# A two-layer transformer kernel: shared tokens in transposed form, keys of several batches in one product, and a re-written order of work

## The chip, the cores and the metric

The kernel runs on one core of one Trainium2 chip. The metric is the device time of one launch in microseconds (us). The core has five engines that run side by side and tell each other by semaphores what is done: TensorE (PE, matrix products, weight loads shown as PEld), VectorE (DVE), ScalarE (ACT), GpSimd (POOL) and SyncE (SP), which here issues every transfer. Each engine works through its own list strictly in the order in which the list was written.

## The reference

```python
xn = layernorm(x)                                   # x: 8 batches x 256 tokens x 128
x  = x + attention(xn, Wq, bq, Wk, bk, Wv, bv, Wo, bo) + experts(xn, Wg, w1, w2)
xn = layernorm(x)
x  = x + state_space(xn, W_in, conv, A, D, W_x, W_dt, W_out) + ffn(xn, w1, w2, h1, h2, w3)
# attention: 16 query heads, 4 key/value heads of 8 columns, softmax over 256 keys
# experts: gates from xn @ Wg, top two of 8; all experts have the same w1 (128x512), w2
# state_space: 4 taps, silu, dt = softplus, and over 512 tokens a row, 16 states a channel:
#   h = h * exp(-A * dt) + B;  y = sum(h) + D * x;  y * silu(z) @ W_out
# ffn: silu(x @ w1.T) * (x @ w2.T), two 512x512 layers with gelu, one 512x128
```

## The kernel before

The first layer (function `layer0`) goes batch by batch, b = 0 to 7, with 256 tokens each. The second (`layer1`) goes group by group, g = 0 to 3, with 512 tokens each. What an engine does is cut into named pieces, and the table `ORDERS` says for each engine in which order the pieces stand; `S` in the tensor list is the next score piece, `A` the next one of the second kind, and so on. There is no scheduler: the tables are the order.

A batch of the first layer takes these pieces on TensorE, by their lines in the kernel before: `xn_transposes` (L444) turns the normalised tokens; `project` (L457 queries, L460 keys) multiplies them by Wq and by Wk; `v_gate` (L431) makes values and gate numbers; 16 `S` pieces (L328, L317 for the first half of batch 0) make scores whose row maxima VectorE takes (`M`, L589); `max_rows` (L423) turns the maxima; 16 `A` pieces (L342) make the scores again, transposed and with the maxima taken off inside the product; ScalarE turns each into probabilities (`E`, L548); four `pv` pieces (L357) multiply them by the values; `heads`, `back` and `proj_out` (L374, L408, L414) bring the result back; `ffn_in` and `ffn_out` (L388, L396) are the experts. Queries and keys are cut into three bfloat16 parts that are written to memory (`put`, L242 and L245) and read back in another layout (`fetch`, L255 and L259, for `S`; `stack`, L283, for `A`). The parts are made by ScalarE (`qk_out`, L521 and L522: four instructions a batch) and GpSimd (`qk_split`, L692 to L695: three). `warm` (L451) are products that nobody reads.

In the second layer `x_in` (L933), `ffn` (L885, L886), `second` (L896), `third` (L908) and `out` (L970, L980) are the large products of a group. For each of 16 states ScalarE makes two decays (`D`, L1088), TensorE spreads the input (`b`, L869), VectorE does two recurrences (`scan`, L1163) and GpSimd adds both to a sum (`add`, L1218). GpSimd closes a group with `y` (L1226), which `out` reads.

Two of the eight banks in which products land serve `S`, two serve `A`, one `pv`. The other three, bA, bB and bC, are shared: bA has the turned tokens in its left half and the two projections in its two halves, bB the experts, bC values, turned maxima and the way back. Before it writes such a bank, each piece waits until the former content is read.

Of the kernel before, what the change touches and what calls it, by code (L numbers as in the profile page):

```python
# [65 lines left out]
def settled(eng, sem, v):  # L66
# [6 lines left out]
    sync="""2*x_in head ffn_weights constants0 x_in 3*put fetch stack 3*put fetch stack 3*put 3*rows fetch loads 2*put  # L73
        rows put 2*rows loads stack fetch 3*rows stack 3*put fetch loads 3*rows 3*put fetch stack 3*rows 3*put fetch
        stack 3*rows put stack 2*put fetch 3*rows stack 3*rows b_rows loads b_rows 2*out 2*b_rows 6*out landed""",
    tensor="""9*warm xn_transposes 4*warm project ffn_in v_gate 6*warm ffn_in 2*S warm xn_transposes S project ffn_out 2*S
        warm S xn_transposes 2*S 4*warm 2*S warm project 2*S 5*warm 2*S 5*warm 2*S warm ffn_in warm max_rows 2*S
        warm ffn_in v_gate 2*S warm ffn_out A S A S 2*warm A S warm A S warm xn_transposes A S A S project 2*S pv S
        2*A S A S A S ffn_in max_rows A S A S pv A S A S pv A S A S ffn_in A S A S pv A S A S v_gate heads ffn_out A
        S xn_transposes back A S A S project S A S pv A S proj_out A S A S max_rows pv A S A S A S v_gate A S A S pv  # L80
        A S A pv A 2*S A heads ffn_in A S A S back ffn_in A S A S pv A S A S xn_transposes proj_out ffn_out max_rows
        A S A S pv A S A project A S A S pv S v_gate A S A S pv A 2*S A heads ffn_in A S A S pv A S A S back ffn_in
        proj_out A S A S xn_transposes ffn_out max_rows A S A S pv A S A S project v_gate ffn_in A S A S pv A S A S
        pv A S A S ffn_in A S A S pv A S A S heads ffn_out back A S A S proj_out xn_transposes A S A S max_rows
        project A S A 2*pv A 2*S A v_gate A S pv A S A S ffn_in A S A S heads A S pv A S A S ffn_in A S A S back
# [1264 lines left out]
```

## Time and profile before

| | us |
|---|---|
| median of three runs (lowest, highest) | 371.38 (370.75, 372.19) |
| span of the profiled execution, first to last instruction | 370.3 |
| the profiled execution's own time outside the span | not listed apart; median less span is 1.1 |
| TensorE busy | 361.6 |
| ScalarE busy | 314.4 |
| VectorE busy | 303.1 |
| GpSimd busy | 238.0 |

A busy TensorE is not a TensorE at its peak: products are pipelined and overlap in the profile. How long a piece really holds the engine is the distance from its start to the start of the next one where nothing is waited for.

### The profile page before, as it was taken

How to read it: one execution, taken by the hardware profiler on the slowest of the kernel's cores; microseconds unless marked ns; L12 is line 12 of the kernel's file. 1: busy time of each engine (PE TensorE's matmuls, PEld its weight loads, DVE VectorE, ACT ScalarE, POOL GpSimd, SP SyncE). 2: the span in 40 equal slices, each digit the busy share in tenths (PEclk: the TensorE clock that was granted, in tenths of full speed). 3: DMA queues.
4: the chain of work that ended last, by engine and by line, in shares of the span. 5: the costliest groups of instructions: out<-in, count | busy, mean ns of one | idle time of the engine just before them, and what ended most of it. 6: DMA issues, size and time to landing. Idle time of an engine off the chain costs nothing.

```text
span 370.3 us, 5874 instructions
## 1 busy us (share of the span) xinstructions
PE 361.6 (98%) x1810; PEld 185.9 (50%) x1810; DVE 303.1 (82%) x508; ACT 314.4 (85%) x540; POOL 238.0 (64%) x287
## 2 busy tenths in 40 slices
PE   7999999999999999999999999999999999999996
PEld 6757454546454553433324445465445464464546
DVE  4786879978788888579878768989999989998950
ACT  4934878886988887899998899999999999799870
POOL 2156504642527211342989673999999999999990
PEclk9999999999999999999969999999999999999999
DMA  6477282746265220220000000001000000000000
GB/s 217 125 145 147 93 200 35 174 143 120 58 110 123 43 55 2 52 85 0 1 21 3 1 0 2 0 0 48 5 0 21 0 3 28 1 2 1 0 28 28
DMA packets 29902, 19.63 MB, mean 53 GB/s; under 512 B 4496, under 2 KB 28848, under 8 KB 29616
## 3 DMA queue, kind: packets, MB, share of 16 engines
q1 hardware_dynamic: 29872, 19.26, 21.3%
q8 instruction: 14, 0.23, 0.3%
q14 instruction: 16, 0.13, 0.1%
HBM read 13.69 MB, written 5.37 MB: 51 GB/s over the span
## 4 chain that ended last, share of the span: by engine, by line
PE 68%; ACT 8%; DMA 2%; issue 2%; DVE 2%; SPq 0%; POOL 0%; ACTq 0%; DVEq 0%; POOLq 0%
PE bank L908 15%; PE bank L896 13%; PE bank L357 6%; PE bank L980 4%; PE bank L342 4%; ACT da L1088 3%; PE bank L869 3%; PE bank L885 3%; PE bank L886 3%; PE bank L953 3%; PE bank L933 3%; PE bank L388 2%; PE bank L328 2%; PE bank L396 2%; PE bank L970 2%; ACT pt L548 2%
## 5 line engine op out<-in xcount | busy, mean ns | idle before, releaser
L1218 POOL TENSOR_TENSOR acc<-acc,hb 128x512 f32<-128x512 f32 x128 | 158.1, 1273 | 11.6 <-DVE hb L1163 11.2
L1163 DVE TENSOR_TENSOR_SCAN hb<-da,bank 128x512 f32<-128x512 f32 x128 | 145.9, 1200 | 15.1 <-PE bank L869 9.1
L589 DVE TENSOR_REDUCE mx<-bank 128x2 f32<-128x512 f32 x128 | 83.1, 683 | 16.9 <-PE bank L328 14.4
L1088 ACT ACTIVATE da<-dt,nega 128x510 f32<-128x510 f32 x128 | 82.2, 713 | 0.2
L548 ACT ACTIVATE pt<-bank 128x512 f32<-128x512 f32 x128 | 71.2, 596 | 9.8 <-PE bank L342 8.7
L896 PE MATMUL bank<-sil,ld 128*128 128x512 f32 x128 | 59.1, 595 | 0.0
L908 PE MATMUL bank<-gelu,ld 128*128 128x512 f32 x128 | 58.5, 593 | 0.1
L342 PE MATMUL bank<-q_st,k_st 51*128 51x512 bf16 x128 | 42.2, 386 | 1.8 <-ACT pt L548 1.5
L328 PE MATMUL bank<-k_st,q_st 48*128 48x256 bf16 x240 | 38.9, 273 | 0.1
L896 PEld LDWEIGHTS bank<-sil,ld 128*128 128x128 f32 x128 | 24.3, 192 | 26.3 <-issue 25.7
L908 PEld LDWEIGHTS bank<-gelu,ld 128*128 128x128 f32 x128 | 23.8, 190 | 25.6 <-issue 24.7
L357 PE MATMUL bank<-pt,v_sb 128*32 128x512 f32 x256 | 35.4, 632 | 0.0
L342 PEld LDWEIGHTS bank<-q_st,k_st 51*128 51x128 bf16 x128 | 9.4, 93 | 38.3 <-ACT pt L548 25.5
L869 PE MATMUL bank<-b_parts,sel 96*128 96x512 bf16 x64 | 24.3, 393 | 0.4 <-DVE hb L1163 0.4
L1088 ACT ACT_TABLE_LOAD x18 | 23.1, 1283 | 0.3
L1142 DVE SCALAR_TENSOR_TENSOR xc<-bank,ld,xc 128x510 f32<-128x510 f32 (+2 forms) x24 | 17.6, 743 | 3.5 <-ACT xc L1015 2.9
L328 PEld LDWEIGHTS bank<-k_st,q_st 48*128 48x128 bf16 x240 | 15.5, 94 | 8.5 <-DVE mx L589 4.8
L692 POOL TENSOR_TENSOR qk_parts<-qk,qk_parts 128x512 bf16<-128x512 f32 x7 | 8.1, 1156 | 16.2 <-ACT qk_parts L522 16.2
L388 PE MATMUL bank<-xnT,w 128*128 128x256 f32 x64 | 17.3, 392 | 0.0
L933 PE MATMUL bank<-xnT,ld 128*128 128x512 f32 x32 | 16.7, 607 | 0.5 <-DVE xc L1142 0.3
L980 PEld LDWEIGHTS bank<-ld,gelu 128*128 128x128 f32 x128 | 15.8, 192 | 2.4 <-issue 2.1
L885 PE MATMUL bank<-xnT,ld 128*128 128x512 f32 x32 | 16.5, 598 | 0.0
(148 smaller groups left out, 534.0 us busy)
## 6 DMA issues: line engine op xcount, KB each, us to landing
q_st<-q_scr SPq DMA_DIRECT2D x8, 384.0 KB, 4.9
q_st<-q_scr SPq DMA_DIRECT2D x15, 192.0 KB, 3.8
ld<-in_pack SPq DMA_DIRECT2D x2, 1024.0 KB, 6.3
q_scr<-qk_parts SPq DMA_DIRECT2D x8, 192.0 KB, 2.1
k_st<-k_scr SPq DMA_DIRECT2D x15, 96.0 KB, 4.5
q_scr<-qk_parts SPq DMA_DIRECT2D x8, 128.0 KB, 2.1
out<-x SPq DMA_DIRECT2D x8, 128.0 KB, 1.9
ld<-in_pack SPq DMA_DIRECT2D x1, 968.0 KB, 5.4
```

Of the source, the lines that this page charges most:

```text
L328: last = mm(s_bank[n % 2][:, j * T:(j + 1) * T], q_st[b % 2][0:ROWS, 2 * pair + j, q * P:(q + 1) * P], k_st[b % 2][0:ROWS, 2 * pair // G, ...
L342: mm(st(b, n)[:, :], k_st[b % 2][HALF:, kv, kt * P:(kt + 1) * P], q_st[b % 2][HALF:, h0:h0 + 2, :].rearrange("r h n -> r (h n)"), start=Tr ...
L357: last = mm(pv_bank[kv * VW:(kv + 1) * VW, :], v_sb[b % 2][:, kt, kv, at:at + VW], pt[:, (4 * grp + kv) % 8, :], start=(grp == 0), stop=(g ...
L548: act(pt[:, n % 8, :], st(b, n)[:, :], ACT.Exp, scale=HD ** -0.5).then_inc(p_ok, 1)
L589: eng.tensor_reduce(mx[:, 2 * pair:2 * pair + 2, q], s_bank[n % 2][:, :].rearrange("p (h k) -> p h k", h=2), AX.X, ALU.max).then_inc(mx_ok, 1)
L869: mm(b_bank(g, s)[:, :], sel[:, s, :], b_parts[:, g % 2, :], start=True, stop=True).then_inc(b_ps, 1)
L896: last = mm(f_bank(g, c)[:, :], h1[:, k, c * P:(c + 1) * P], sil[:, k, :], start=(k == 0), stop=(k == KC - 1))
L908: last = mm(f_bank(g, c)[:, :], h2[:, k, c * P:(c + 1) * P], g2[:, k, :], start=(k == 0), stop=(k == KC - 1))
L980: last = mm(out_bank(g, q)[:, r], g3[:, k, r], w3[:, k, :], start=False, stop=(k == KC - 1 and q == out_last(g, q)))
L1088: act(da(n)[:, :, 1:T], dt[:, g % 2, c, :].rearrange("p (b n) -> p b n", b=GB)[:, :, 1:T], ACT.Exp, scale=nega[:, c, s:s + 1]).then_inc(da ...
L1163: eng.tensor_tensor_scan(hb[:, s % NPAIR, c, :], da(n).rearrange("p b n -> p (b n)"), b_bank(g, s)[:, :], 0.0, ALU.mult, ALU.add).then_inc ...
L1218: TT(acc[:, g % 2, c, :], acc[:, g % 2, c, :], hb[:, s % NPAIR, c, :], ALU.add).then_inc(add_ok, 1)
```

## The change

The normalised and turned tokens of all eight batches now stay in the buffer `xnT1`, which the second layer fills later, so that their making can run ahead; `xn` has two buffers. The keys of batch 0, of batches 1 to 3 and of batches 4 to 7 are made by one piece each, `project_keys`: one product of 32 columns of weights for each batch, side by side in one bank. Key parts are made, cut and written for the whole group (`k_out`, `split_k`, `put_keys`), query parts for each batch (`q_out`, `split_q`, `put`). There are four value buffers instead of two. The semaphores of fetched data are kept apart for even and odd batches. Turned tokens and queries use the left half of one bank (`half0`), values, maxima and the way back the right half of another (`half1`); the two halves of the tokens' bank are no longer both used. Which content must be read before a shared bank is written stands in short tables (`X_AFTER` to `H_AFTER`). The first loads come in another order and size. All five lists of `ORDERS` are new. The score banks stay one bank for each piece, two in turn.

```diff
-    sync="""2*x_in head ffn_weights constants0 x_in 3*put fetch stack 3*put fetch stack 3*put 3*rows fetch loads 2*put
+    sync="""2*x_in head constants0 x_in ffn_weights put_keys 2*put 2*put_keys put fetch 2*put_keys 2*put put_keys put
...
+NV = 4
+KEYS = ((0,), (1, 2, 3), (4, 5, 6, 7))
+X_AFTER = "- q0 x1 x2 q1 q2 x5 x6"
+Q_AFTER = "x0 x3 x4 k2 q3 q4 q5 q6"
+KEYS_AFTER = "x7"
+V_AFTER = "- m0 m1 m2 m3 m4 m5 m6"
+M_AFTER = "v0 v1 v2 p1 p2 v5 p4 v7"
+T_AFTER = "v3 p0 v4 v6 p3 m7 h6 h7"
+P_AFTER = "t0 t1 t2 t3 t4 t5 t6 t7"
+F_AFTER = "- f0 f1 h1 h2 f4 h3 h4"
+H_AFTER = "f2 h0 f3 f5 f6 f7 p5 p6"
...
-    xnT = [sb(f"xnT_{p}", [P, T]) for p in range(2)]
-    xn = sb("xn", [P, TPB, P])
+    xnT = [t["xnT1"][:, b * T:(b + 1) * T] for b in range(NB)]
+    xn = [sb(f"xn_{p}", [P, TPB, P]) for p in range(2)]
...
-    X_PARTS = ((0, TPB), (TPB, 3 * TPB), (3 * TPB, NT))
+    bA, bB, bX = banks[5:8]
+    half0, half1 = bA[:, 0:T], bX[:, T:2 * T]
+    X_PARTS = ((0, TPB), (TPB, 4 * TPB), (4 * TPB, NT))
...
+    EMPTIED = dict(x=((xnT_ok, 1),), q=((q_ok, 1),), k=((k_ok, 1),), v=((v_ok, 1), (srt_ok, TPB)), m=((negm_ok, 1),),
+                   t=((oT_ok, 1),), p=((x1_ok, 1),), h=((on_ok, 1),), f=((y_ok, 1),))
+    def emptied(eng, before, n):
+        name = before.split()[n]
+        if name == "-":
+            return
+        for signal, per in EMPTIED[name[0]]:
+            eng.wait_ge(signal, per * (int(name[1:]) + 1))
...
+        def put_keys(n):
+            j, k = n // NRUN, n % NRUN
+            first, last = KEYS[j][0], KEYS[j][-1]
+            k_out = a["k_scr"][first:last + 1].rearrange("o p c n -> (o p) c n")
...
         def project(b):
             reached(eng, xnT_ok, b, 1, 1)
-            mm(bA[:, 0:T], wq[:, :], xnT[b % 2][:, :], start=True, stop=True)
+            emptied(eng, Q_AFTER, b)
+            mm(half0, wq[:, :], xnT[b], start=True, stop=True).then_inc(q_ps, 1)
...
-            mm(bA[:, T:2 * T], wk4[:, :], xnT[b % 2][:, :],
-               start=True, stop=True).then_inc(qk_ps, 1)
+        def project_keys(j):
+            reached(eng, xnT_ok, KEYS[j][-1], 1, 1)
...
+            for i, b in enumerate(KEYS[j]):
+                last = mm(key_bank(j)[32 * i:32 * i + 32, :], wk4[:, 0:NKV * HD], xnT[b], start=True, stop=True)
+            last.then_inc(k_ps, 1)
...
         def xn_out(b):
             reached(eng, xnT_ps, b, 1, 1)
-            reached(eng, f_ps, b - 2, 1, 1)
-            reached(eng, v_ps, b - 2, 1, 1)
-            act(xnT[b % 2][:, :], bA[:, 0:T], ACT.Copy).then_inc(xnT_ok, 1)
+            act(xnT[b], half0, ACT.Copy).then_inc(xnT_ok, 1)
...
-        def qk_out(b):
-            for half, bias in ((0, bq_c), (1, bk_c)):
+        def q_out(b):
+            if b > 0:
+                act(qk[:, 0:T], half0, ACT.Identity, bias=bq_c[:, 0:1])
+            act(qk_parts[:, 0, 0:T], half0, ACT.Identity, bias=bq_c[:, 0:1]).then_inc(q_ok, 1)
+        def k_out(j):
+            r = slice(0, NKV * HD * len(KEYS[j]))
+            if j > 0:
+                act(qk[r, T:2 * T], key_bank(j)[r, :], ACT.Identity, bias=bk_c[r, 0:1])
+            act(qk_parts[r, 0, T:2 * T], key_bank(j)[r, :], ACT.Identity, bias=bk_c[r, 0:1]).then_inc(k_ok, 1)
...
-            reached(eng, pv_ok, b - 2, 4, 4)
+            reached(eng, pv_ok, b - NV, 4, 4)
...
-        def qk_split(b):
-            TT(qk_parts[:, 1, :], qk[:, :], qk_parts[:, 0, :], ALU.subtract).then_inc(split, 1)
+        def split_q(b):
+            c = slice(0, T)
+            TT(qk_parts[:, 1, c], qk[:, c], qk_parts[:, 0, c], ALU.subtract).then_inc(q_split, 1)
```

Three places show how the lists move. The first is TensorE at the start of the second layer's share of batch 7; `L342` is the `A` piece, `L357` `pv`, `L933` `x_in`, `L885` and `L886` `ffn`. Before:

```order
L423 MATMUL bank<-head,mx 32x128
L342 MATMUL bank<-q_st,k_st 128x512 x2
L357 MATMUL bank<-pt,v_sb 32x512 x4
L342 MATMUL bank<-q_st,k_st 128x512
L357 MATMUL bank<-pt,v_sb 32x512 x4
L342 MATMUL bank<-q_st,k_st 128x512 x2
L933 MATMUL bank<-xnT,ld 128x512
```

After, where the same pieces are L402, L417, L1008, L959 and L960, and L461 and L468 are `back` and `proj_out`:

```order
L402 MATMUL bank<-q_st,k_st 128x512
L994 MATMUL bank<-head,xn 128x128 x4
L943 MATMUL bank<-b_parts,sel 128x512
L417 MATMUL bank<-pt,v_sb 32x512 x4
L402 MATMUL bank<-q_st,k_st 128x512
L1008 MATMUL bank<-xnT,ld 128x512 x2
L402 MATMUL bank<-q_st,k_st 128x512
L468 MATMUL bank<-cst,oT 128x128 x2
L417 MATMUL bank<-pt,v_sb 32x512 x4
L402 MATMUL bank<-q_st,k_st 128x512
```

The end of batch 5 (`back`, `proj_out`) and the `pv` pieces now stand between the `A` pieces of batch 7, which are spread more evenly.

The second place is ScalarE where the second layer's group 1 begins its recurrences; `da` is a decay `D`, `xc` the taps. Before:

```order
L1015 ACTIVATE xc<-bank,ld 128x512
L1088 ACT_TABLE_LOAD
L1088 ACTIVATE da<-dt,nega 128x2x255
L1015 ACTIVATE xc<-bank,ld 128x512
L1088 ACTIVATE da<-dt,nega 128x2x255
L1009 ACT_TABLE_LOAD
L1009 ACTIVATE sil<-bank,ld 128x512
```

After:

```order
L1090 ACTIVATE xc<-bank,ld 128x512 x2
L1084 ACT_TABLE_LOAD
L1084 ACTIVATE sil<-bank,ld 128x512
L1117 ACTIVATE xn<-x,nmean,rstd 128x128 x4
L1097 ACTIVATE zs<-bank 128x512
L1084 ACTIVATE sil<-bank,ld 128x512
L1097 ACTIVATE zs<-bank 128x512
L1084 ACTIVATE sil<-bank,ld 128x512
L1108 ACTIVATE xs<-xc 128x512 x2
L1084 ACTIVATE sil<-bank,ld 128x512
L1163 ACT_TABLE_LOAD
L1163 ACTIVATE da<-dt,nega 128x2x255 x2
```

The first two decays of group 1 moved behind the last `sil`, and one table load is gone there.

The third is GpSimd at the same place; `acc<-xs` is `start`, the other `acc` are `add`. Before:

```order
L1218 TENSOR_TENSOR acc<-acc,hb 128x512 x4
L1226 TENSOR_TENSOR y<-acc,zs 128x512 x2
L1210 TENSOR_TENSOR acc<-xs,ld 128x512
L1218 TENSOR_TENSOR acc<-acc,hb 128x512 x9
L1231 TENSOR_TENSOR b_rest<-b_full,b_cut 128x128
```

After:

```order
L1302 TENSOR_TENSOR y<-acc,zs 128x512
L1294 TENSOR_TENSOR acc<-acc,hb 128x512
L1286 TENSOR_TENSOR acc<-xs,ld 128x512
L1302 TENSOR_TENSOR y<-acc,zs 128x512
L1294 TENSOR_TENSOR acc<-acc,hb 128x512 x3
L1307 TENSOR_TENSOR b_rest<-b_full,b_cut 128x128
```

The `start` ahead of group 1's adds is now one of group 1 itself; before, it was one of group 2.

## Rows read from the trace of the kernel before

**Rows 1.** The page: busy times, 40 slices of the span, the chain by engine.

```profile
PE 361.6 (98%) x1810; PEld 185.9 (50%) x1810; DVE 303.1 (82%) x508; ACT 314.4 (85%) x540; POOL 238.0 (64%) x287
...
PEclk9999999999999999999969999999999999999999
...
PE 68%; ACT 8%; DMA 2%; issue 2%; DVE 2%; SPq 0%; POOL 0%; ACTq 0%; DVEq 0%; POOLq 0%
```

**Rows 2.** Timeline of TensorE: start, length, line, operation, shape, count, [idle before].

```profile
5.72 0.44 PE L444 MATMUL bank<-head,xn 128*128 128x128 f32 x2 [0.73 <-DMA head<-in_head]
...
14.59 0.59 PE L457 MATMUL bank<-xnT,head 128*128 128x256 f32 x2
15.02 0.59 PE L460 MATMUL bank<-xnT,head 128*128 128x256 f32 x2
...
30.06 0.27 PE L423 MATMUL bank<-head,mx 128*32 128x128 f32 x1
...
42.12 0.39 PE L342 MATMUL bank<-q_st,k_st 51*128 51x512 bf16 x1 [0.47 <-ACT pt L548]
...
46.41 1.06 PE L357 MATMUL bank<-pt,v_sb 128*32 128x512 f32 x8
47.41 0.39 PE L342 MATMUL bank<-q_st,k_st 51*128 51x512 bf16 x1
...
47.95 1.13 PE L388 MATMUL bank<-xnT,w 128*128 128x256 f32 x4
```

**Rows 3.** Timeline of TensorE: where batch 7 and the second layer's stages begin.

```profile
149.73 0.39 PE L342 MATMUL bank<-q_st,k_st 51*128 51x512 bf16 x1
...
186.92 0.61 PE L342 MATMUL bank<-q_st,k_st 51*128 51x512 bf16 x1 [0.15 <-ACT pt L548]
...
216.05 1.88 PE L933 MATMUL bank<-xnT,ld 128*128 128x512 f32 x4
...
361.97 1.95 PE L970 MATMUL bank<-wout_half,y 128*128 128x128 f32 x16
```

**Rows 4.** Busy time by stage: stretch, length, PE, PEld, DVE, ACT, POOL, clock.

```profile
149.70:186.90 37.20, 35.51 (x142) 13.62 (x141) 28.51 (x37) 36.12 (x63) 20.44 (x22) 0.98 0.11 34
231.90:361.70 129.80, 129.80 (x438) 66.07 (x436) 117.82 (x115) 122.65 (x167) 128.26 (x109) 1.00 0.03 10
...
188.00:190.00 2.00, 2.00 (x12) 0.39 (x8) 1.14 (x2) 1.97 (x3) 2.00 (x2) 0.50 0.22 49
```

**Rows 5.** Groups by line, ScalarE and GpSimd: busy, mean ns, idle before.

```profile
L522 ACT ACTIVATE qk_parts<-bank,cst 128x256 bf16<-128x256 f32 x16 | 7.5, 474 | 0.0
...
L1088 ACT ACT_TABLE_LOAD x18 | 23.1, 1283 | 0.3
```

**Rows 6.** Timeline of ScalarE around the end of batch 7 and at group 1.

```profile
39.91 0.47 ACT L521 ACTIVATE qk<-bank,cst 128x256 f32<-128x256 f32 x1
...
41.47 2.16 ACT L548 ACTIVATE pt<-bank 128x512 f32<-128x512 f32 x4
...
188.18 1.28 ACT L1069 ACT_TABLE_LOAD   x1
189.47 1.27 ACT L1069 ACTIVATE gelu<-bank,ld 128x512 f32<-128x512 f32 x2
...
219.20 0.72 ACT L1088 ACTIVATE da<-dt,nega 128x510 f32<-128x510 f32 x1
```

**Rows 7.** Timeline of GpSimd from group 1's adds on.

```profile
227.96 1.04 POOL L1210 TENSOR_TENSOR acc<-xs,ld 128x512 f32<-128x512 f32 x1 [8.41 <-ACT xs L1033]
...
231.93 8.65 POOL L1218 TENSOR_TENSOR acc<-acc,hb 128x512 f32<-128x512 f32 x7 [0.46 <-DVE hb L1163]
...
359.13 2.49 POOL L1226 TENSOR_TENSOR y<-acc,zs 128x512 f32<-128x512 f32 x2
```

**Rows 8.** The chain that ended last, around batch 6's fetch: start, length, what.

```profile
102.56 4.87 DMA q_st<-q_scr
```

**Rows 9.** Timeline of VectorE: the second pair of recurrences of group 1.

```profile
230.63 11.40 DVE L1163 TENSOR_TENSOR_SCAN hb<-da,bank 128x512 f32<-128x512 f32 x10 [1.26 <-ACT da L1088]
```

More of the change, by code:

```diff
@@ L72 @@
 ORDERS = dict(
-    sync="""2*x_in head ffn_weights constants0 x_in 3*put fetch stack 3*put fetch stack 3*put 3*rows fetch loads 2*put
[L74 to L85, printed above, removed]
-        ffn_out A S proj_out pv max_rows S A S A ffn_in A S A S pv A S v_gate A S A S pv A S A S ffn_in heads A S A
-        S pv S A x_transposes A S A S back ffn_out A S A S x_in proj_out x_in ffn max_rows 2*A pv A pv 2*A x_in ffn
-        x_in A wx A ffn 2*step_in ffn b A x_transposes pv A x_in b x_in A 2*second heads b A x_in A second x_in A b
-        second wx pv A b step_in back A pv A b step_in A b A proj_out 2*A b A 2*pv 2*b 2*second b second b second
-        heads b third back third proj_out b 2*third 2*b 3*third x_transposes third 2*x_in 2*ffn x_in 2*b x_in 2*ffn
-        out wx b 2*second b second b 2*second b second out b step_in b 2*second 2*b 3*out third b out x_transposes b
-        third x_in step_in 2*b 2*third b third b 2*third b x_in third x_in 2*ffn b x_in wx b 2*ffn step_in b out b
-        2*second b second b second b 2*second b second b second 2*out b out b 2*out third b third step_in b third b
-        third b third b third b 2*third b ffn b ffn out b ffn b ffn out b 2*out second b 2*second b second b second
-        b second b 2*second b 2*out b 2*third b 2*third b 4*third 6*out""",
@@ L119 @@
[L119 to L122 removed]
+    sync="""2*x_in head constants0 x_in ffn_weights put_keys 2*put 2*put_keys put fetch 2*put_keys 2*put put_keys put
+        fetch put stack 2*rows 2*put rows fetch loads stack put_keys 3*rows 2*put put_keys put loads fetch stack put
+        put_keys 2*put 3*rows 3*put fetch stack 3*rows fetch stack 3*put 3*rows fetch stack loads 3*rows 2*put stack
+        put fetch 3*rows stack 3*rows loads 2*b_rows 2*out 2*b_rows 6*out landed""",
@@ L302, in ffn_weights @@
             eng.dma_start(w12[:, :], a["w12"]).then_inc(ld_ffn, 16)
-        return dict(x_in=x_in, head=head, constants0=constants0, ffn_weights=ffn_weights, put=put, fetch=fetch, rows=rows,
+        return dict(x_in=x_in, head=head, constants0=constants0, ffn_weights=ffn_weights, put=put, put_keys=put_keys, fetch=fetch, rows=rows,
                     stack=stack, loads=loads)
@@ L1179, in clear @@
                 settled(eng, done["st_ps"], (NB - 1) * NH)
-                settled(eng, done["stk_ok"], 32 * NB)
+                for p in range(2):
+                    settled(eng, done["stk_ok"][p], 16 * NB)
                 settled(eng, done["y_ok"], NB)
```

323 lines of the change are left out of this document (183 added, 140 removed).

## The prediction, made before the changed kernel had run

> **What bounds the kernel now.** I read the page first, then TensorE's own timeline, then the busy time by stage, then the lists of ScalarE and GpSimd. On the page TensorE is busy for 361.6 of 370.3 us and makes up 68% of the chain that ended last, with its clock at 2.4 GHz but for one slice [rows 1]. A busy share hides how much of it is work, so I priced each piece by the distance from its start to the next start where nothing is waited for: one projection 0.43 us (14.59 to 15.02), `pv` 1.00 (46.41 to 47.41), and two `A` with two `S` beside them 0.54 (47.41 to 47.95), that is 0.21 for each pair and 0.1 for leaving the small-tile form [rows 2]. Pieces of `ffn_in`, `ffn_out` and the second layer are priced in the same way: 0.86 for each product of 512 columns in float32, 0.11 for one of 128. Multiplied by the pieces in the list before, this makes 348.3 us of work. The remaining 22 us of the span are idle time of TensorE or half-speed time, and they are what a new order can win.
>
> By stages, each ended by a row: the first `max_rows` at 30.06 [rows 2], the first `A` of batch 7 at 149.73, its last `A` at 186.92, `x_in` of group 2 at 216.05 and the last group's `out` at 361.97 [rows 3].
>
> - To 30.06: 26.1 us of work, 4.0 idle (the first loads; `xn_transposes` waits for a load until 5.72 [rows 2]).
> - To 149.73: 112.0 of work, 7.7 idle, in dozens of waits of 0.1 to 0.9 us.
> - To 186.92: 33.8 of work in 37.2. Here ScalarE is busy 36.1 of 37.2 us [rows 4]: it is the bound of this stage.
> - To 216.05: 26.2 of work, 2.9 lost, most of it at half clock: between 188 and 190 us the granted clock is 0.50 of full speed [rows 4], just after `A` pieces for which TensorE had waited for ScalarE, the last at 186.92 [rows 3].
> - To 361.97: 144.8 of work, 1.1 idle. TensorE is stall-free from about 232 on, but GpSimd is busy for 128.3 of the 129.8 us from 231.9 to 361.7 [rows 4]. Both are the bound: the last two `y` end at 361.62, and the `out` that reads them starts at 361.97 [rows 3, 7].
> - The last 8.3 us (24 products, an add, a transfer) don't change.
>
> **The change part by part.**
>
> *Keys.* Eight key projections of 0.43 us go (3.4 us of TensorE). Three groups of 1, 3 and 4 products of 32 weight columns come. The trace has no such product of 256 columns, but `pv` is four products of 32 columns side by side: eight passes in 1.00 us [rows 2], which one after the other would be at least four times 0.86. If key products overlap in the same way, the three groups cost 3 x 0.43 = 1.3; if not, 8 x 0.43 = 3.4, and nothing is won. I take 1.3, since the form of `pv` is the same. Range of the edit: -2.1 to 0.
>
> *Form changes.* Counting both lists, TensorE leaves or enters the small-tile form 146 times instead of 138, at 0.1 us: +0.8. The Trainium skill (TensorEngine Tiling (Array Packing), Key Properties) says that a change of tiling mode drains the engine while different tiles run in parallel; the trace agrees with both halves, at 0.1 us a change and with `pv` as above, and the first half speaks against this change. With the keys the work falls from 348.3 to 347.0.
>
> *ScalarE.* Four conversions a batch (0.47 us each, 0.36 apart) become two, and three groups of one or two are added. In the old order the four stand in a row between two `E`: they begin at 39.91, the next `E` at 41.47 [rows 6], and TensorE's `A` at 42.12 had waited for it [rows 2]. Seven such gaps of 1.5 us become 0.7. Of the table loads of 1283 ns [rows 5], 49 in the list before, 40 are left: 11.5 us less over the whole kernel. The Trainium skill (ScalarE: Activation LUTs, What ACT_TABLE_LOAD costs) adds a drain of about 1.38 us to each load, which would make 24 us; the trace doesn't show it here: the load at 188.18 is followed by its `gelu` at 189.47 [rows 6].
>
> *GpSimd and transfers.* Cutting goes from 3 x 1.16 us on 512 columns to three on 256 for each batch, and four `put` transfers a batch less are issued. In the old order batch 6's fetch landed at 107.43 [rows 8], while TensorE wanted it 0.3 us before. In the new one the queries of batches 4 to 7 are projected 25, 29, 26 and 22 us of work ahead of their scores (before 18, 14, 13 and 16). Price -0.5. On SyncE `rows` of batch 0 now stand behind two `put` of batch 2; these are due some 2 us before the maxima are, so I take 0, up to +1.
>
> *Start.* The second load of x grows from 256 to 384 KB ahead of the weights that `xn_transposes` waits for, and the experts' weights become the last load. I expect the first transposition near 6.2 instead of 5.72 and `ffn_in` near 9.6 instead of 8.2; the two stretches of `warm` ahead of it shrink by about as much. The first `S` comes at 11.3 to 12.0 (before 11.57). Price 0, -0.3 to +1.
>
> *Value buffers, parity semaphores.* Before, making values of batch b waited for `pv` of b-2, which cost VectorE 0.4 us in all. Hidden beside TensorE's work: 0.
>
> *New waits.* All small results now pass through two half banks. Behind each such wait stands the whole of TensorE's list. The distances in work between writer and next writer are at least 0.7 to 1.1 us at the tightest (values of batches 1, 3 and 7 after maxima, and `max_rows` of batch 6), about what the reads between them take (0.25 to 0.4 us and a handover). So 0 to 0.3 each, some 1 us in all.
>
> *Stage sums.* With the new list the stages hold 26.1, 107.9, 37.1, 25.7 and 144.8 us of work: four us move from the second stage past the first `A` of batch 7. For idle time I take 4.0 in the first stage. In the second, 6.0 (7.7 less 0.5 for the fetch, less about 2 for the shorter ScalarE rows, plus 1 for new waits). In the third, ScalarE's list between first and last `E` of batch 7 falls from 36.5 to 35.0 us, below TensorE's 37.1: TensorE becomes the bound, with 1.2 idle. In the fourth I take 1.6 instead of 2.9, half-way between keeping and losing the half-speed stretch, which cost about 2.5.
>
> In the fifth the end is set by GpSimd. The first two decays of group 1 move behind the last `sil`; they were made at 219.20, between the taps [rows 6]. By the chain taps, x_in, ffn, sil, table load (1.28), decay, I get the first recurrence of group 1 at 229.4 on the old clock instead of 225.75, the second pair at 231.7 instead of 230.63 [rows 9], and the first add at 230.6. From there GpSimd's list holds 132.5 us with no hole, so the last `y` ends at 363.1 instead of 361.6: +1.5. What is won is that the add no longer waits for group 2's `start`, which had cost 8.41 us of GpSimd idling until 227.96 [rows 7].
>
> Sum: 30.1 + 113.9 + 38.3 + 27.3 + (144.8 + 1.1 + 1.5) + 8.3 = 365.3 us of span, against 370.3. With the 1.1 us by which the median stands over the span: 366.4.
>
> **The rivals.**
>
> *More is won (20%).* The half-speed stretch goes altogether (-1.6) and the second stage loses only 4 us (-2): 362.8. For it: TensorE would no longer wait for ScalarE ahead of that stretch. Against it: `A` pieces still come one by one between waits.
>
> *Given back on GpSimd (18%).* Recurrences of group 1 start yet later, since the decays stand behind a `sil` that needs the last `ffn` product, and everything after is a full GpSimd list: each microsecond there is one of the end. With +3.5 instead of +1.5 and the second stage unchanged at 7.7: 370.1. This includes key products that don't overlap (+2).
>
> *The half banks bind (12%), slower.* `v_gate`, `max_rows`, `back` and `proj_out` share one half bank, each released by VectorE or ScalarE from the middle of its own full list. If VectorE comes 0.5 us late at three of them a batch, eight batches lose 12 us, less the gain of 5.0: 378. It decides from about 0.3 us a time on. For it: VectorE is busy for 303 of 370 us [rows 1], so a short read often stands behind longer work of its list. Against it: the shorter ScalarE rows let scores and probabilities, for which VectorE's list waits too, come on time more often.
>
> *The change doesn't do what it says.* If no piece ran earlier and only the work fell, 1.3 us are won: 370.1, within the second rival.
>
> **How the numbers follow.** Forecast 50%, its own range 363.8 to 369.0. A measurement of this kernel can tell 0.5%, or 1.9 us, from no change: faster means below 369.5. The forecast and the first rival lie there, and a third of the second's half-way cases, less the forecast's upper tail: 0.71. Within 0.5% lie most of the second rival and the mild form of the third: 0.18. Slower: 0.11. The range of 8 in 10 leaves out a tenth on either side: 362.3 to 373.0.
>
> **What would show it.** In the changed profile: key products of a group starting within about 0.1 us of each other, and each group done in some 0.45 us; the last `A` of batch 7 near 182; ScalarE less than fully busy in the stage before it; 40 table loads; no or a shorter stretch at 0.50 clock after it; the first add of group 1 near 225 and GpSimd without a hole from there to the last `y` near 357. Wrong, if TensorE's waits for `half1` (VectorE's copies and adds on the way back, the maxima) add up to over 3 us, if the first `A` of batch 7 comes after 147, or if GpSimd has new holes after group 1's first add.

## The result: slower by 1.2%, and the profile after

| | before | after |
|---|---|---|
| median (us) | 371.58 (370.75 to 372.19, 4 runs) | 375.97 (375.85 to 376.16, 4 runs) |
| ratio after to before | | 1.0124, 95% interval 1.0101 to 1.0146 |
| span of the profiled execution | 370.3 | 374.4 |
| its own time | not listed | 376.16 |

The forecast of 366.4 and its range (362.3 to 373.0) missed. The page of the changed kernel, answering to [rows 1]: ScalarE is relieved as forecast (314 to 298 us), but 15% of the chain that ended last is now "issue", time in which an engine in the chain waited for nothing that the profile shows.

```profile
PE 364.5 (97%) x1810; PEld 184.7 (49%) x1810; DVE 303.1 (81%) x514; ACT 298.0 (80%) x521; POOL 232.0 (62%) x293
...
PEclk9999999999999999999999999999989999999998
...
PE 61%; issue 15%; ACT 13%; POOL 6%; DVE 3%; POOLq 0%; ACTq 0%; DVEq 0%
```

The timeline of TensorE (start, length, line, operation, shape, count, what ended its idle time) shows where the stages of [rows 2, 3] end now, and two places that were not there before.

```profile
7.35 0.38 PE L492 MATMUL bank<-head,xn 128*128 128x128 f32 x2
...
16.78 0.63 PE L518 MATMUL bank<-xnT,head 128*32 128x256 f32 x6
17.34 1.12 PE L375 MATMUL bank<-hb,dt 128*128 128x512 f32 x2
...
31.18 0.27 PE L475 MATMUL bank<-head,mx 128*32 128x128 f32 x1
...
146.28 0.39 PE L402 MATMUL bank<-q_st,k_st 51*128 51x512 bf16 x1
...
185.10 0.39 PE L402 MATMUL bank<-q_st,k_st 51*128 51x512 bf16 x1
...
212.46 1.96 PE L1008 MATMUL bank<-xnT,ld 128*128 128x512 f32 x4
...
272.36 1.02 PE L960 MATMUL bank<-xnT,ld 128*128 128x512 f32 x2
275.69 1.23 PE L959 MATMUL bank<-xnT,ld 128*128 128x512 f32 x2 [2.31 <-DVE sil L1200]
276.71 1.92 PE L960 MATMUL bank<-xnT,ld 128*128 128x512 f32 x2
278.42 2.71 PE L1045 MATMUL bank<-wout_half,y 128*128 128x128 f32 x16
...
364.33 2.84 PE L1045 MATMUL bank<-wout_half,y 128*128 128x128 f32 x16 [1.91 <-POOL y L1302]
366.96 4.59 PE L1055 MATMUL bank<-ld,gelu 128*128 128x128 f32 x32
```

Stage by stage, in us:

| stage up to | before | forecast | after |
|---|---|---|---|
| first `max_rows` | 30.1 | 30.1 | 31.2 |
| first `A` of batch 7 | 119.7 | 113.9 | 115.1 |
| last `A` of batch 7 | 37.2 | 38.3 | 38.8 |
| `x_in` of group 2 | 29.1 | 27.3 | 27.4 |
| last group's `out` | 145.9 | 147.4 | 151.9 |
| end | 8.3 | 8.3 | 10.1 |

(The row names follow the prediction; the fourth ends with the `x_in` at 216.05 before and 212.46 after.) The gain of the first layer and of its seam came: 216.05 became 212.46. Then 3.6 us in hand became 4.1 us lost. Of that, 6.0 us went before the last `out` and 1.7 us behind it. About half of the 3.6 us is clock: the profiled execution of before has a half-speed stretch in the fourth stage that cost 1.8 us and that the same order does not always have (e5 below).

At the first new place TensorE waits for `sil`. ScalarE's timeline shows who held that up:

```profile
268.68 0.69 ACT L1084 ACTIVATE sil<-bank,ld 128x512 f32<-128x512 f32 x1 [0.15 <-PE bank L960]
273.15 0.60 ACT L1097 ACTIVATE zs<-bank 128x512 f32<-128x512 f32 x1 [3.79 <-POOL y L1302]
273.65 0.62 ACT L1108 ACTIVATE xs<-xc 128x512 f32<-128x512 f32 x1
274.17 0.68 ACT L1084 ACTIVATE sil<-bank,ld 128x512 f32<-128x512 f32 x1
```

`zs` is `gate_z` of group 3's first half. It writes a buffer that group 1's `y` reads, and its wait asks for both `y` of group 1. GpSimd's timeline has them late in a list without holes, and then holes:

```profile
269.21 1.27 POOL L1302 TENSOR_TENSOR y<-acc,zs 128x512 f32<-128x512 f32 x1
270.44 1.27 POOL L1294 TENSOR_TENSOR acc<-acc,hb 128x512 f32<-128x512 f32 x1
271.79 1.27 POOL L1302 TENSOR_TENSOR y<-acc,zs 128x512 f32<-128x512 f32 x1
...
277.44 1.27 POOL L1294 TENSOR_TENSOR acc<-acc,hb 128x512 f32<-128x512 f32 x1 [0.93 <-DVE hb L1238]
...
284.46 2.50 POOL L1294 TENSOR_TENSOR acc<-acc,hb 128x512 f32<-128x512 f32 x2 [1.07 <-DVE hb L1238]
288.06 1.27 POOL L1294 TENSOR_TENSOR acc<-acc,hb 128x512 f32<-128x512 f32 x1 [1.10 <-DVE hb L1238]
...
361.59 2.48 POOL L1302 TENSOR_TENSOR y<-acc,zs 128x512 f32<-128x512 f32 x2
```

The circle is closed: ScalarE waits for GpSimd's `y`, TensorE for the `sil` queued behind that wait, VectorE's recurrences for TensorE's `b`, GpSimd for the recurrences. Before the change the same `y` ended at about 273.5 and ScalarE came to the same `zs` at 273.89, so nobody waited:

```profile
271.04 2.48 POOL L1226 TENSOR_TENSOR y<-acc,zs 128x512 f32<-128x512 f32 x2
...
273.89 0.59 ACT L1022 ACTIVATE zs<-bank 128x512 f32<-128x512 f32 x1
```

GpSimd moved only 0.5 us forward (to 273.06), ScalarE 4.5 (to 269.36). Against an execution of the old order without the half-speed stretch (e5: `y` ends at 271.71, `zs` begins at 272.04) ScalarE moved 2.7 us forward and GpSimd 1.35 us back.

Both waits of TensorE are followed by slow products. Busy time by stretch (length, then PE, PEld, DVE, ACT, POOL, the granted clock as the sixth number, DMA share, GB/s):

```profile
275.60:282.90 7.30, 7.21 (x37) 5.63 (x38) 6.39 (x8) 6.92 (x8) 6.38 (x6) 0.77 0.00 0
364.30:371.00 6.70, 6.67 (x45) 6.70 (x46) 0.00 (x0) 0.00 (x0) 0.00 (x0) 0.75 0.00 0
```

Sixteen `out` records take 2.54 us from 278.42 to the next piece instead of the 1.78 that the same piece took before (361.97 to 363.75): part of them run at 1.2 GHz.

### The profile page after: what moved, and what is told of

Same layout as the page of the kernel before. It is cut to its first block, busy times and chain, and to the rows that moved or that the text cites. A ratio compares the mean times of both kernels' runs of the same rounds, so it can differ in the third digit from the quotient of the medians.

```text
span 374.4 us, 5851 instructions
## 1 busy us (share of the span) xinstructions
PE 364.5 (97%) x1810; PEld 184.7 (49%) x1810; DVE 303.1 (81%) x514; ACT 298.0 (80%) x521; POOL 232.0 (62%) x293
## 4 chain that ended last, share of the span: by engine, by line
PE 61%; issue 15%; ACT 13%; POOL 6%; DVE 3%; POOLq 0%; ACTq 0%; DVEq 0%
PE bank L970 7%; PE bank L417 7%; PE bank L402 5%; ACT da L1163 5%; POOL acc L1294 4%; PE bank L386 4%; PE bank L445 4%; PE bank L453 4%; PE bank L499 4%; PE bank L982 4%; PE bank L1055 3%; DVE hb L1238 2%; PE bank L960 2%; PE bank L959 2%; PE bank L1045 2%
## 5 line engine op out<-in xcount | busy, mean ns | idle before, releaser
L402 PE MATMUL bank<-q_st,k_st 51*128 51x512 bf16 x128 | 40.8, 383 | 0.3 <-ACT pt L612 0.3
L417 PE MATMUL bank<-pt,v_sb 128*32 128x512 f32 x256 | 34.1, 605 | 0.0
L402 PEld LDWEIGHTS bank<-q_st,k_st 51*128 51x128 bf16 x128 | 9.0, 93 | 36.4 <-ACT pt L612 25.9
L943 PE MATMUL bank<-b_parts,sel 96*128 96x512 bf16 x64 | 23.5, 382 | 0.1
L959 PE MATMUL bank<-xnT,ld 128*128 128x512 f32 x32 | 16.8, 605 | 2.3 <-DVE sil L1200 2.3
L1055 PEld LDWEIGHTS bank<-ld,gelu 128*128 128x128 f32 x128 | 17.1, 202 | 3.6 <-issue 3.4
L1055 PE MATMUL bank<-ld,gelu 128*128 128x128 f32 x128 | 17.2, 284 | 0.0
L960 PE MATMUL bank<-xnT,ld 128*128 128x512 f32 x32 | 17.2, 621 | 0.0
L499 PE MATMUL bank<-warm_in 128*128 128x256 bf16 x88 | 15.9, 317 | 1.4 <-DVE warm_in L622 1.4
```

The source lines that it names most:

```text
L402: mm(st(b, n)[:, :], k_st[b % 2][HALF:, kv, kt * P:(kt + 1) * P], q_st[b % 2][HALF:, h0:h0 + 2, :].rearrange("r h n -> r (h n)"), start=Tr ...
L417: last = mm(pv_bank[kv * VW:(kv + 1) * VW, :], v_sb[b % NV][:, kt, kv, at:at + VW], pt[:, (4 * grp + kv) % 8, :], start=(grp == 0), stop=( ...
L1055: last = mm(out_bank(g, q)[:, r], g3[:, k, r], w3[:, k, :], start=False, stop=(k == KC - 1 and q == out_last(g, q)))
```

## The experiments

**e1 and e5: the wait for `y`.** The same edit to the changed kernel and to the kernel before.

```diff
         def gate_z(g, c):
-            reached(eng, y_ok, g - 2, CI, CI)
+            reached(eng, y_ok, g - 2, CI, c + 1)
```

> One edit to the changed kernel: the gate z of group g waits only for the y of its own half that last read the buffer, not for both y of group g-2. Theory (the gain of the first layer is lost in the second, where ScalarE stands 3.8 us before zs at 273.15 for GpSimd's y): TensorE's idle 2.3 us at 275.69 and the slow products behind it (1.8 us) shrink to under 0.5 together, GpSimd's three holes of about 1 us each between 277 and 289 go, the last y ends near 361 instead of 364.07, and the span is 371 to 371.5 (time about 373). TensorE then waits longer for the last y, about 3 us instead of 1.9. Rival (the time was lost in the first layer on the shared half banks): span unchanged within 0.5 us.

> The kernel before the change with the same one edit as e1 (gate z waits only for the y of its own half). Theory (the wait costs only in the new order, in which ScalarE comes to zs at 269.4 while GpSimd's second y ends at 273.1; in the old order both met at 273.5 and 273.9): no change, span 370.3 within 0.5, ratio 1.00. Rival (the wait cost the old order as well, and e1 is a gain of its own and no loss of the change): the span falls by 2 us or more, to about 368.

Measured: e1 371.24 us, ratio to before 0.9991 (0.9974 to 1.0008), span 370.0; e5 371.15 us, ratio 0.9994 (0.9971 to 1.0017). One number in one wait takes back the whole loss of the changed kernel, 4.4 us of span and 4.7 of the median, at least 1 us more than I expected, and is worth nothing in the old one. (e5's profiled span of 368.5, below the forecast 370.3, is that of an execution without the half-speed stretch of [rows 4]; its median is that of the kernel before.) In e1 ScalarE still waits, but for 1.20 and 0.89 us, and TensorE does not:

```profile
270.49 0.60 ACT L1097 ACTIVATE zs<-bank 128x512 f32<-128x512 f32 x1 [1.20 <-POOL y L1302]
270.98 0.62 ACT L1108 ACTIVATE xs<-xc 128x512 f32<-128x512 f32 x1
271.50 0.68 ACT L1084 ACTIVATE sil<-bank,ld 128x512 f32<-128x512 f32 x1
273.07 0.60 ACT L1097 ACTIVATE zs<-bank 128x512 f32<-128x512 f32 x1 [0.89 <-POOL y L1302]
```

The three holes of GpSimd between 277 and 289 are gone, and its last `y` ends at 359.72 instead of 364.07. e1's rival, a loss in the first layer, is refuted; so is e5's, that the edit is a gain of its own. At the end TensorE waits 1.88 us for the last `y` (I expected 3), and the products behind it are slow as in the changed kernel.

Why is e1 still not faster than the kernel before, when that was forecast? e5's profile is the old order (its edit changes nothing there) with the clock at full speed throughout TensorE's work, and it answers this stage by stage (us):

| stage up to | old order (e5) | forecast for the new | new order, wait mended (e1) |
|---|---|---|---|
| first `max_rows` | 30.0 | 30.1 | 31.1 |
| first `A` of batch 7 | 120.0 | 113.9 | 115.1 |
| last `A` of batch 7 | 37.0 | 38.3 | 38.8 |
| `x_in` of group 2 | 27.3 | 27.3 | 27.4 |
| last group's `out` | 145.9 | 147.4 | 147.6 |
| end | 8.4 | 8.3 | 10.0 |

With its wait mended the fifth stage takes what was forecast. The fourth is as long in both orders: what it gained over the kernel before is the half-speed stretch alone, which none of the 15 profiled executions of the new order has. And GpSimd's list, full in both, begins 0.5 us later and ends at the same time (359.77 and 359.72). First e5, then e1 (`x_in` of group 2, first add of group 1, last `y`, last `out`):

```profile
214.21 1.88 PE L933 MATMUL bank<-xnT,ld 128*128 128x512 f32 x4
227.13 2.50 POOL L1218 TENSOR_TENSOR acc<-acc,hb 128x512 f32<-128x512 f32 x2
357.28 2.49 POOL L1226 TENSOR_TENSOR y<-acc,zs 128x512 f32<-128x512 f32 x2
360.13 1.95 PE L970 MATMUL bank<-wout_half,y 128*128 128x128 f32 x16
...
212.37 1.95 PE L1008 MATMUL bank<-xnT,ld 128*128 128x512 f32 x4
227.65 3.74 POOL L1294 TENSOR_TENSOR acc<-acc,hb 128x512 f32<-128x512 f32 x3 [10.83 <-DVE hb L1238]
357.24 2.48 POOL L1302 TENSOR_TENSOR y<-acc,zs 128x512 f32<-128x512 f32 x2
359.98 2.79 PE L1045 MATMUL bank<-wout_half,y 128*128 128x128 f32 x16 [1.88 <-POOL y L1302]
```

From `x_in` to the first add it is 12.9 us in the old order and 15.3 in the new one (forecast 14.6), so the 1.8 us that TensorE is ahead at `x_in` never reach GpSimd.

**e10: order alone.** The waits stay; `gate_z` moves behind the next `sil`.

```diff
-  ... 4*hid gate_x sil gate_z gate_x sil gate_z 2*D     (ScalarE)
+  ... 4*hid gate_x sil gate_x sil 2*gate_z 2*D
-  ... 2*scan conv scan mul zm mul zm 2*scan             (VectorE)
+  ... 2*scan conv scan 2*mul 2*zm 2*scan
```

> The changed kernel with its waits as they are and only the order of ScalarE and VectorE altered at one place: gate z of group 3's first half moves behind the next sil (sil, gate x, gate x, sil, gate z, gate z, and mul, mul, zm, zm on VectorE). Theory (the loss comes from where the piece stands, a wait that both kernels have): the fourth pair of ffn products no longer waits 2.3 us, no holes on GpSimd, span 370 to 370.5 as in e1. Rival (the wait for y holds up ScalarE wherever gate z stands, as two sil follow it still): at most half of the 4.4 us comes back.

Measured 372.07 us, ratio 1.0009 (0.9991 to 1.0027), span 370.9: 3.5 of 4.4 us come back, so the rival (at most half) is refuted. ScalarE still waits 2.08 us for `y`, but what TensorE needs stands ahead of that wait; only the next two `sil` are late, for which TensorE waits 0.24 us at 281.03. So it is the place of the piece in the list that costs, together with the width of its wait.

**e2, e3: the tail.** Products that nobody reads ahead of the wait for the last `y`; e3 has e1's edit too.

```diff
+                if g == NG - 1:
+                    for _ in range(16):
+                        mm(out_bank(g, 0)[:, 0:P], ident[:, :], ident[:, :], start=True, stop=True)
                 reached(eng, y_ok, g, CI, CI)
```

> One edit to the changed kernel: 16 products of 128 columns that nobody reads stand between the waits for the banks and the wait for the last y, so that TensorE stays busy in the 1.9 us in which it waits for y. Theory (the tail is long because the granted clock falls after that idle time): the last group's out still starts near 364.3, but the 48 products behind it end in about 5.3 us as before the change instead of about 6.8, and the span is 372.7 to 373.1 (time about 374.4). Rival (the products are slow for another reason, or the idle time is only moved): no change in the tail, or slower by the length of the products.

> Both edits of the two kernels above. If the two losses are independent they add: span 374.4 less 3.1 less 1.6, some 369.7 (time about 371.3, the same as the kernel before the change). If 16 products (1.8 us) no longer fill a wait of 3 us for y, part of the clock's 1.6 us stays and the span is 370.5 to 371.

Measured: e2 375.70 us, span 374.1; e3 371.54, span 369.5. My size was off: such a product counts twice in the trace (x32) and takes 0.22 us, so the 16 lasted 3.57 us and `out` began at 365.73, 1.4 us later than in the changed kernel. Yet the end came 0.3 us earlier. The clock's part is as forecast:

```profile
365.70:371.00 5.30, 5.30 (x50) 5.30 (x48) 0.16 (x1) 0.00 (x0) 0.00 (x0) 1.00 0.01 3
```

From the first `out` to VectorE's sum it is 5.1 us here (365.73 to 370.84) and 6.8 in the changed kernel (364.33 to 371.14): 1.7 us of the tail are half-speed time behind 1.9 us of waiting. As a remedy the unread products are worth nothing: they end later than `y` comes, and the medians are 375.70 against 375.97 and, with e1's edit, 371.54 against 371.24.

**e14, e8, e12: products that don't need `y` first.** In the last group the 12 products of three chunks of the experts go ahead of the 8 that read `y`; all three have e1's edit. e8 has e6's start besides, e12 e9's (both below).

```diff
+            late = g == NG - 1
+            if late:
+                n = (1, 2, 3, 0, 4, 5)[n]
```

> The changed kernel with three edits: gate z waits for its own y (as e1), the loads of e6, and in the last group the 12 products of the experts' first three chunks ahead of the 8 that need the last y. Theory: e1's span 370.0, less 0.8 for the loads, less 1.35 for the products that now fill most of the 2 us in which TensorE waits for y, less up to 1.6 for the clock that stays at full speed: 366.3 to 367.5 (time about 368.3, ratio 0.992). Rival (the idle time before y is long enough even so for the clock to fall): 368.

> All that is expected to help: gate z waits for its own y (e1), the last group's 12 products ahead of those that need y (e8), and the start of e9. In e8 the first max_rows came at 32.3 and the span was 367.5; with the first max_rows near 30.3 the whole list is 2 us earlier: span 365.3 to 366.3, time about 367.3, ratio 0.989 to the kernel before. Rival (the start's gain is lost on the way, as GpSimd sets the end): span 367 to 367.5.

> The changed kernel's start unaltered, with gate z waiting for its own y and, in the last group, the 12 products of the first three chunks ahead of those that need y. Both e8 and e12 had a first max_rows at 32.3 and 32.7, later than the changed kernel's 31.18, and spans of 367.5 and 367.9. Theory (what the start loses, the end loses in full): span 366.2 to 366.8, time about 368.2. Rival (GpSimd's end swallows it): 367.3 or more.

Measured: e8 369.22 us, ratio 0.9940 (0.9912 to 0.9969); e12 369.42, 0.9944 (0.9931 to 0.9957); e14 367.80, 0.9889 (0.9874 to 0.9904), span 366.0. In e14 TensorE has no idle time at the end, and its clock does not fall:

```profile
350.81 7.03 PE L982 MATMUL bank<-gelu,ld 128*128 128x512 f32 x16
357.68 2.84 PE L1061 MATMUL bank<-ld,gelu 128*128 128x128 f32 x24
360.35 1.95 PE L1051 MATMUL bank<-wout_half,y 128*128 128x128 f32 x16
362.14 1.06 PE L1061 MATMUL bank<-ld,gelu 128*128 128x128 f32 x8
```

The last `y` still ends where it did (359.51 in e14, 359.72 in e1). What e14 gains on e1, 4.0 us of span, is mostly the wait of 1.9 us and the 1.7 us of half-speed time behind it. e8's time is 0.9 us above its forecast and e12's 2.1 us: their starts came late. The first `max_rows` came at 32.30, 32.67 and 30.88 in e8, e12 and e14, the span ended at 367.5, 367.9 and 366.0.

**e4, e6, e9, e13: the start.** The first `max_rows` is 1.1 us late. Four tries, each from what the one before showed: e4 has fewer unread products, e6 also the experts' weights earlier, e9 also another place for VectorE's moments, e13 splits the last part of x (and keeps the changed kernel's other loads).

```diff
-    tensor="""15*warm xn_transposes ...                 (e4, e6, e9: 11; e13: 12)
-    sync="""2*x_in head constants0 x_in ffn_weights     (e6, e9)
+    sync="""2*x_in head ffn_weights constants0 x_in
-    vector="""... clear_values moments 2*first_split    (e9)
+    vector="""... clear_values 2*first_split moments
-    X_PARTS = ((0, TPB), (TPB, 4 * TPB), (4 * TPB, NT))                          (e13)
+    X_PARTS = ((0, TPB), (TPB, 4 * TPB), (4 * TPB, 6 * TPB), (6 * TPB, NT))
```

> One edit to the changed kernel: 11 pairs of unread products ahead of the first transposition instead of 15 (before the change there were 9). Theory (the first transposition at 7.35 waits for these and not for its loads, and the 1.1 us by which the first max_rows is late comes from there): the first transposition at 5.8 to 6.2, the first max_rows 0.7 to 1.2 us earlier than 31.18; the whole list moves up, so the span falls by about as much, to 373.2 to 373.8. Rival (the chain of loads, ScalarE's copies and key conversions sets the first stage): max_rows unchanged within 0.3 us. A second rival: it arrives earlier but GpSimd's y still sets the end through ScalarE's wait, and half of the gain is lost there.

> The changed kernel with the experts' weights loaded third again, ahead of the constants and of the last part of x, and with 11 pairs of unread products at the start. Theory (the first max_rows is 1.1 us late since ffn_in waits for the experts' weights, which land last): ffn_in at 8.6 to 9.2 instead of 10.17, the first max_rows at 29.9 to 30.5 instead of 31.18, last A of batch 7 near 184.2. The wait for y in group 2 is set by GpSimd, which moves up too, so the span is 373.2 to 373.7. Rival (the last part of x comes later and ScalarE's normalised tokens of batches 4 to 7 with it): no gain at the first max_rows, a wait at xn_transposes of a later batch.

> e6's edits (experts' weights loaded third, 11 pairs of unread products) and VectorE cuts the first queries and keys before it takes the moments of the last eight tiles of x; ScalarE's deviation of these tiles moves behind two normalisations. Theory (in e6 TensorE's second transposition waited 1.4 us, until 12.07, for the cutting of the queries in the same half bank, which stood on VectorE behind moments that waited for the last part of x): the second transposition at 10.4 to 10.9, the first max_rows at 29.8 to 30.6 instead of 31.18, and the span 373.2 to 373.8. Rival (another link of the start chain is right behind): max_rows stays above 30.9.

> The changed kernel with the last part of x in two (four and four tiles; the second lands last and its moments stand on VectorE behind the first four maxima), and 12 instead of 15 pairs of unread products at the start. Theory (the start is set by VectorE: 2.3 us of moments of eight tiles ahead of the cutting of the first queries, behind whose half bank the second transposition waits): the cutting begins 1.2 to 1.8 us earlier than 10.55, the second transposition at 10.2 to 10.7 instead of 11.72, the first max_rows at 30.0 to 30.7 instead of 31.18, the span 373.4 to 373.9. Rival (as in e9, the moments hold up something wherever they stand): the first max_rows at 31 or later.

Measured, first `max_rows` and time: e4 31.80 and 375.88; e6 31.77 and 376.69; e9 32.70 and 376.78; e13 30.45 and 373.81 (372.20 to 376.51). The spans are 374.9, 374.8, 374.2 and 371.6: the first three are above their forecasts, and e13's is below its own since the clock did not fall behind the wait for `sil` in this execution. In e4 the first transposition did come at 5.84, but `ffn_in` then waited for the experts' weights until 10.42. In e6 `ffn_in` began at 8.93 and the second transposition waited instead:

```profile
12.07 0.41 PE L492 MATMUL bank<-head,xn 128*128 128x128 f32 x2 [1.42 <-DVE qk_rest L728]
```

The second transposition uses the half bank of batch 0's queries, which VectorE reads to cut them. VectorE's timeline in the changed kernel has that cutting behind the moments of eight tiles, 2.3 us:

```profile
8.31 1.65 DVE L633 BATCH_NORM_STATS2 bst<-x_sb 128x6 f32<-128x128 f32 x8 [0.63 <-DMA x_sb<-in_x]
10.00 0.64 DVE L636 BATCH_NORM_AGGREGATE mv<-bst 128x2 f32<-128x6 f32 x8
10.55 0.46 DVE L728 SCALAR_TENSOR_TENSOR qk_rest<-bank,cst,qk_parts 128x256 f32<-128x256 f32 x1
```

In e9 the cutting stands first and the maxima wait for the moments (TensorE's third score product waits 1.88 us). With the moments in two lumps (e13) the cutting began at 9.76 and the second transposition at 10.51. So three things lie close together at the start: the unread products, the experts' weights (e4) and VectorE's moments (e6). Take one away, and the next one holds TensorE up. In the changed kernel's own profile it is the unread products: the first transposition comes at 7.35 behind them, and from there to the second one at 11.72 the profile lists no wait of TensorE. The eight profiled executions that have this start (the changed kernel, e1, e2, e3, e7, e10, e11, e14) have their first `max_rows` between 30.79 and 31.29, so e13's 30.45 brings back 0.3 to 0.8 us of the 1.1.

**e15: all that helped.** e14 with e13's start.

> e14 with the start of e13. Theory: what e13 gains at the first max_rows (0.5 to 1.1 us) comes off e14's span one for one: 365.3 to 366.0. Rival: the same as e14 within 0.3, as GpSimd's list, which begins with recurrences that other waits set, ends at the same time.

Measured 367.19 us, ratio 0.9881 (0.9862 to 0.9900), span 365.2, the fastest; e14 and it are 8.2 and 8.8 us below the changed kernel. The first `max_rows` came 0.53 us earlier than in e14 (30.35) and the span ended 0.8 us earlier: 0.5 us is no more than such executions differ by, but with e8 and e12 there are four pairs, from 30.35 and 365.2 to 32.67 and 367.9, in which start and end move together within a few tenths.

**e7: a half bank of its own for the way back.**

```diff
+    def way_back(b):
+        return bA[:, T:2 * T] if b <= 4 else half1
-M_AFTER = "v0 v1 v2 p1 p2 v5 p4 v7"
+M_AFTER = "v0 v1 v2 v3 v4 v5 v6 v7"
-T_AFTER = "v3 p0 v4 v6 p3 m7 h6 h7"
+T_AFTER = "- p0 p1 p2 p3 m7 h6 h7"
```

> The changed kernel with the way back (back, proj_out) of batches 0 to 4 in the free right half of the tokens' bank, so that it no longer takes turns with values and turned maxima. My third rival said that these turns bind. Theory (they hardly do): TensorE's idle time between the first max_rows and the first A of batch 7 falls from 7.1 us by 0 to 0.6. Rival (half banks bind): it falls by 2 us or more, and the first A of batch 7 starts near 144 instead of 146.28. The span stays within 0.5 us of 374.4 unless the rival holds.

Measured 375.76 us, span 374.2; the stage takes 114.97 us (31.12 to 146.09) instead of 115.10, so 0.1 us of TensorE's idle time goes. The turns that the way back takes do not bind; values and turned maxima still share a half bank here, and that was not tried apart.

**e11: the first decays of group 1 early.** e1 with them ahead of the `sil` pieces.

```diff
-  ... 2*taps sil normalise gate_z sil gate_z sil 2*gate_x sil 2*D b_in 20*D   (ScalarE)
+  ... 2*taps 2*D sil normalise gate_z sil gate_z sil 2*gate_x sil b_in 20*D
-  ... 2*scan 2*conv 2*mul 2*zm 2*mul 8*scan                                  (VectorE)
+  ... 2*scan 2*conv scan 2*mul 2*zm 2*mul 7*scan
```

> e1 with the first two decays of group 1 back ahead of the sil pieces, directly behind the taps, and the first pair of recurrences directly behind VectorE's taps. My prediction's step: their move behind the last sil costs 1.5 us at GpSimd's end. Theory (GpSimd's list has no hole, so an earlier first add is an earlier end): first add at 221 to 222 instead of 227.7, the last y 1 to 2 us earlier than in e1 (359.7), span 368.3 to 369.3 against e1's 370.0. Rival (one more table load and two decays, 2.6 us, delay the sil pieces, TensorE's second layer waits some 2 us for them and its clock may fall): span 370 to 371.5.

Measured 372.29 us, ratio 1.0029 (1.0011 to 1.0048): the rival. The first adds come at 219.83, but the third only at 231.59 (GpSimd idle for 9.27 us), the last `y` ends at 361.56 instead of e1's 359.72, and TensorE waits 1.76 us for `sil` at 221.56. `b_in` now stands in the way of the third decay as well, so this is not exactly the old arrangement, and it does not show what the move of the two decays alone costs.

## Why the prediction was wrong

**The fifth stage, priced at 1.1 us idle plus 1.5 for GpSimd, is the step that failed.** Its loss over the 144.8 us of work was forecast as 2.6 us and measured as 7.1. I wrote that from the first add "GpSimd's list holds 132.5 us with no hole" and added its delay to TensorE's sum. The first add came at 227.73; 132.5 us later is 360.2, and the last `y` ended at 364.07, so 3.8 us of holes. What I left out is that a list that gains time runs into the one that does not: I followed which pieces GpSimd needs from the others, but not who waits for GpSimd's `y` in the middle of the stage. ScalarE did, at `gate_z` of group 3, which the old order reached 0.4 us behind `y` and the new one 3.8 us ahead of it. e1 and e10 show it: 4.4 and 3.5 us of span. With e1's edit the list does hold no more than was forecast (132.1 us from 227.65 to 359.72), and the stage takes 147.6 us, forecast 147.4.

**The end "doesn't change"** also failed, by 1.7 us. Before, TensorE worked up to 361.97 and `y` ended at 361.62; TensorE waited for nothing there, and the tail ran at full clock. I did forecast that GpSimd would be the bound, from which a wait of TensorE at the end follows, and did not price what it does to the clock. e2 measures it: 1.7 us.

**The start, priced at 0 (range to +1), cost 1.1.** The step "the two stretches of `warm` ahead of it shrink" was misread: the list has 15 pairs ahead of the first transposition where it had 9, so that it came at 7.35, not 6.2. Close behind it stand the experts' weights (e4) and VectorE's moments ahead of the half bank's release (e6), which I had not followed, so that fewer unread products alone bring nothing back.

**The gain ahead of the second layer was forecast too large.** Group 2's `x_in` was to come 6.4 us earlier, at 209.6; it came 3.6 us earlier, and only 1.8 us earlier than in e5. The start lost 1.1 us against the forecast and the second stage 1.2: its idle time is 7.2 us instead of 6.0 (my own terms, 7.7 less 0.5 less 2 plus 1, add up to 6.2), spread over many short waits, and no run took it apart. So the last `A` of batch 7 came at 185.1 and not near 182, and the first add of group 1 at 227.73 and not near 225. The half-speed stretch, which began at about 185.3 and so ahead of the wait at 186.92 that I named, and which I priced at about 2.5 us and took to be half kept, cost 1.8 us in the kernel before (29.1 us in the fourth stage against 27.3 in e5) and is gone in the new order; that the stage takes the 27.3 us forecast all the same is luck, as it loses 1.7 us over its 25.7 us of work with the clock at full speed.

**Right:** the third and fourth stage within 0.5 us, the fourth by luck; TensorE's waits for ScalarE's probabilities in batch 7's stage, down from 0.9 to 0.3 us; 40 table loads; key products that overlap: three of them take 0.56 us together (16.78 to 17.34), where three projections would take 1.3. The Trainium skill (TensorEngine Tiling (Array Packing), Key Properties) says that different tiles run in parallel, and this row agrees. Of the three signs of being wrong one came: new holes of GpSimd behind group 1's first add. The first `A` of batch 7 came at 146.28, ahead of 147.

**The rivals.** The half banks as I put them (three late reads a batch, 378 us) did not bind as far as e7 tries them; the other half bank held TensorE up at the start of e6, for 1.42 us. "Given back on GpSimd" (18%, 370.1) named the right engine and a part of the mechanism. The later decays do make GpSimd's first add later, 15.3 us behind `x_in` instead of 12.9, where I had taken 14.6; by the rows of e1 and e5 this is why e1 gains nothing on the kernel before. That the changed kernel is 4.4 us slower still is another thing, a wait for GpSimd's result by the engine that had gained. Putting the decays back ahead of `sil` did not help (e11, 1.0 us slower than e1). A wrong conversion hid a part: I added 1.1 us to the span, while 15 of the 16 profiled executions since have their own time 1.75 to 1.86 us above their span. By that the profiled execution of before took 372.1 us, about the longest of its four runs (372.19), with a stretch at 0.50 clock [rows 4] that e5's does not have (span 368.5 for the same order).

e15's 367.2 us lie in the forecast's own range (363.8 to 369.0), but not for the forecast's reasons. Its last `out` begins at 359.55 where 357.0 was forecast, and its end takes 5.7 us instead of 8.3, since the 12 products that stand ahead of the wait for `y` no longer stand behind it. The new order by itself, with its one wait mended, is worth nothing (e1, ratio 0.9991).

## What to carry to other kernels

When a new order moves some engines forward by some microseconds, list every wait on an engine that is already full and so will not move, and compare the two times: a wait that was met by 0.4 us before is the new bound, and what stands behind it on its list decides the price. A gain ahead of an engine whose list is full is worth only as much as it brings that list's first piece forward. A wait should ask for the one result that it needs, and work that needs no late result goes ahead of the wait for it. The price of a wait of TensorE is its length plus, often, the slow clock behind it.
